# Unread products between the last steps of a four-layer network's kernel, and its final products moved between the steps of a scan

## What is computed

```python
x = L0(x, ctx, mask)        # 16-head attention, feed-forward of 1024
x = L1(ctx, x)              # attention over ctx, a narrow feed-forward of 4, attention on itself
x = L2(x, ctx)              # causal 16-head attention, feed-forward of 1024
# L3: 8-head attention, then a scan over the 128 positions:
x = x + mha(layernorm(x), layernorm(ctx))
u = (layernorm(x) @ W_in.T + b_in) @ Bmat            # 16 x 128 x 64
s_t = silu(s_{t-1} @ A.T) + u_t                      # for t = 0 .. 127, s_{-1} = 0
x = x + s @ Cmat                                     # 64 -> 256
x = x + (programme.mean(axis=1) @ W_prog.T + b_prog)[:, None, :]
```

## Time and profile before

| | |
|---|---|
| median of three runs | 906.49 us |
| the profiled execution's own time | 904.56 us |
| its span, first to last instruction | 902.4 us |
| mean granted clock of TensorE | 0.905 |
| TensorE busy | 762.0 us (84%) |
| VectorE busy | 538.9 us (60%) |
| ScalarE busy | 432.9 us (48%) |
| GpSimd busy | 336.2 us (37%) |
| end of layer C's last drive product to the end | 107 us |

### The profile page before, as it was taken

One profiled execution on the slowest core, in us unless ns is written; L12 is line 12 of the kernel. 1 busy time (PEld: TensorE's weight loads), 2 busy tenths in 40 slices (PEclk: granted clock), 3 DMA queues, 4 the chain that ended last, 5 costly groups with the idle time before them and its releaser, 6 DMA issues.

```text
span 902.4 us, 16307 instructions
## 1 busy us (share of the span) xinstructions
PE 762.0 (84%) x5520; PEld 615.8 (68%) x5520; DVE 538.9 (60%) x2244; ACT 432.9 (48%) x1768; POOL 336.2 (37%) x343
## 2 busy tenths in 40 slices
PE   0699897899799979997999899979899887575556
PEld 0588676688678868886888788857787666344445
DVE  2547678647847884788478947883776473310002
ACT  0635265665553855385538554872465461312221
POOL 3224354434524553454345524652356151100000
PEclk9889998999999999999999999999999889555556
DMA  8400000000000000000000000000000000010002
GB/s 316 179 7 7 24 9 11 4 11 1 19 1 13 1 20 1 13 1 19 1 13 1 14 1 13 1 2 1 1 1 2 0 2 1 0 24 0 1 1 93
DMA packets 14709, 18.73 MB, mean 21 GB/s; under 512 B 3485, under 2 KB 12194, under 8 KB 13986
## 3 DMA queue, kind: packets, MB, share of 16 engines
q1 hardware_dynamic: 14626, 17.69, 6.0%
HBM read 15.59 MB, written 2.10 MB: 20 GB/s over the span
## 4 chain that ended last, share of the span: by engine, by line
PE 68%; DVE 17%; issue 5%; ACT 5%; POOL 3%; DMA 2%; SPq 0%; DVEq 0%; POOLq 0%
PE work_bank L564 21%; PE work_bank L555 20%; PE work_bank L693 6%; PE scores_bank L763 6%; DVE probs L903 4%; DVE probsT L1004 4%; PE work_bank L613 3%; PE work_bank L547 3%; PE scores_bank L591 3%; ACT probs L1145 3%; DVE xn L921 2%; DVE stats L940 1%; DMA bias<-in_mask 1%; ACT probs L1082 1%; POOL probs L786 1%
## 5 line engine op out<-in xcount | busy, mean ns | idle before, releaser
L786 POOL TENSOR_TENSOR probs<-probs,rtotal 128x512 f32<-128x512 f32 x160 | 164.5, 1040 | 219.4 <-DVE rtotal L994 219.1
L1082 ACT ACTIVATE probs<-probs,nmx 128x128 f32<-128x128 f32 x512 | 197.9, 390 | 77.4 <-DVE nmx L903 77.1
L1004 DVE COPY probsT<-work_bank 128x512 f32<-128x512 f32 x160 | 106.4, 679 | 19.2 <-PE work_bank L693 19.0
L693 PE MATMUL work_bank<-ident,probs 128*128 128x128 f32 x640 | 99.2, 296 | 20.9 <-POOL probs L786 14.5
L564 PE MATMUL work_bank<-L_w,hidden 128*128 128x256 f32 x512 | 113.9, 381 | 0.0
L693 PEld LDWEIGHTS work_bank<-ident,probs 128*128 128x128 f32 x640 | 78.2, 151 | 40.5 <-POOL probs L786 21.6
L564 PEld LDWEIGHTS work_bank<-L_w,hidden 128*128 128x128 f32 x512 | 96.0, 190 | 14.1 <-ACT hidden L1137 1.7
L786 POOL TENSOR_TENSOR rstd<-veps,half 128x2 f32<-128x2 f32 x64 | 45.4, 710 | 160.3 <-DVE veps L948 159.9
L1082 ACT ACTIVATION_READ_ACCUMULATOR probs<-probs,nmx 128x1 f32 x512 | 96.7, 189 | 0.0
L763 PE MATMUL scores_bank<-probs,a_t 64*64 64x16 f32 x252 | 49.6, 276 | 33.3 <-ACT probs L1145 33.3
L763 PEld LDWEIGHTS scores_bank<-probs,a_t 64*64 64x64 f32 x252 | 36.0, 203 | 46.8 <-ACT probs L1145 46.8
(11 more groups left out here) (162 smaller groups left out, 1430.7 us busy)
## 6 DMA issues: line engine op xcount, KB each, us to landing
L_w<-in_L_w SPq DMA_DIRECT2D x4, 1024.0 KB, 10.7
x_in<-in_x SPq DMA_DIRECT2D x8, 256.0 KB, 2.8
c_in<-in_ctx SPq DMA_DIRECT2D x8, 256.0 KB, 2.8
out<-x_all SPq DMA_DIRECT2D x8, 256.0 KB, 2.2
rows<-in_rows SPq DMA_DIRECT2D x1, 1280.0 KB, 8.1
bias<-in_mask SPq DMA_DIRECT2D x8, 128.0 KB, 2.2
L_wq<-in_L_wq SPq DMA_DIRECT2D x3, 256.0 KB, 9.6
L_wv<-in_L_wv SPq DMA_DIRECT2D x3, 256.0 KB, 10.1
```

The costliest lines, as they stand in the source:

```text
L693: mm = nc.tensor.transpose(d[:, j * P:j * P + P], src[:, j, :], ident[:])
L786: return nc.gpsimd.tensor_tensor(out, a0, a1, op)
L1004: nc.vector.tensor_copy(turn_slot(s, i, key), d[:].rearrange("p (j k) -> p j k", j=4))\
L1082: ins = nc.scalar.activation(e_at[slot][:, j, :], src, ACT.Exp, bias=nmx[:, slot, j:j + 1], scale=1.0 if s == "C" else -1.0, accum_out=tot ...
```

## The change

1. `occupy` issues products of 128x128 on 128 columns whose results nobody reads. A table `OCCUPIED` puts 8, 2, 8, 8 and 3 of them before C7.flip.x6, C7.q, C7.turn.0, C7.flip.x7 and C7.drive, in the bank which that step then overwrites. In the scan one follows each step before step 99.
2. Of the four L750 products only the first stands before the scan; the others follow steps 8, 40 and 72.
3. The programme is loaded with the weights, last in `REST_LOADS` (into `x7_all`, rows 8 to 11, which are free then). Its means are made with `drive_weight`, and VectorE copies them there.
4. The end's products are split. Positions 0 to 95 ("early") need states up to 95 only: 32 products of 96x128 (`early_part`), one after each step from 99 on, the last three after the scan. For positions 96 to 127 ("late") the batches stand four abreast, 32 partitions each, in a tile `late` (in `probsT`): 32 narrow products (`late_part`) with the inputs and means alone at every fourth step from 13 to 41, and 16 with `w_state` after the last step. SP moves the last 32 rows of `x7_all` into `late` by four transfers.
5. Pairs' stores carry 96 positions and start during the scan; the late ones are four stores, two by SP and two by ScalarE's queue. `w_state` of step 0 is written, and so Silu's table loaded, after C7.out's products.

```diff
@@ pe
+            def occupy(d, n):
+                for _ in range(n):
+                    nc.tensor.matmul(d, wq["L0"][:, 0, 0:P], wk["L0"][:, 0, 0:P], start=True, stop=True,
+                                     skip_group_check=True)
...
+                for b in range(B):
+                    mm = nc.tensor.matmul(d[SS:P, 2 * P + b:2 * P + b + 1], prog[:, b, :], mean_w[:], start=True, stop=True)
                 mm.then_inc(set_up_pe, 1)
...
+                if (s, i, step) in OCCUPIED:
+                    occupy(open_bank(s, i, step)[:, 0:P], OCCUPIED[s, i, step])
...
+            mm = from_u(0)
             for t in range(1, P):
...
                 mm.then_inc(stepped, 1)
+                if t in (8, 40, 72):
+                    from_u(t // 32 + 1)
+                elif t < FROM:
+                    occupy(s_bank[3][:, 3 * P:4 * P] if t < 72 else s_bank[0][:, 0:P], 1)
+                if t == 12:
+                    for w in range(W_BANKS):
+                        pe.wait_ge(drained[w], len(range(w, len(FILLS), W_BANKS)))
+                    pe.wait_ge(late_ready, 1)
+                if 12 <= t < 44 and t % 4 == 1:
+                    late_part((t - 12) // 4)
+                if t >= FROM:
+                    early_part(t - FROM)
+            pe.wait_ge(silued, P - 1)
+            for g in range(4):
+                for j in range(4):
+                    mm = nc.tensor.matmul(s_bank[g // 2][32 * j:32 * j + 32, (g % 2) * D:(g % 2) * D + D],
+                                          w_state[:, EARLY:P, 4 * g + j], w_last[0:SS, :], start=True, stop=True)
+                if g % 2:
+                    mm.then_inc(late_filled, 1)
+            for k in range(P - FROM, 2 * B):
+                early_part(k)
@@ sp
+            sp.wait_ge(*summed_at("C", NT - 1, "x7b"))
+            for j in range(4):
+                sp.dma_start(late[32 * j:32 * j + 32, :, :],
+                             x7_all[EARLY:P, :, :].rearrange("p (g j) d -> p g j d", j=4)[:, :, j, :])\
+                    .then_inc(late_moved, 16)
+            for n in range(NT):
+                sp.wait_ge(last_added, n + 1)
+                sp.dma_start(out[bass.ds(n * PAIR, PAIR), 0:EARLY]..., x7(n)[0:EARLY]).then_inc(out_stored, 16)
+            for j in (0, 1):
+                sp.wait_ge(late_added, 4)
+                sp.dma_start(out[:, EARLY:P]...[j], late[32 * j:32 * j + 32]).then_inc(out_stored, 16)
@@ act
-            act.wait_ge(stepped, 1)
-            nc.scalar.mul(w_state[:, 0, :], u_all[:, 0, :], 0.0)
+            act.wait_ge(*filled_at("C", NT - 1, "out"))
+            nc.scalar.activation(w_state[:, 0, :], zero[:], ACT.Silu)
```

More of the change, by code:

```diff
@@ L245 @@
 W_BANKS, S_BANKS = 4, 4
+EARLY, FROM = 96, 99
+OCCUPIED = {("C", NT - 1, ("flip", "x6")): 8, ("C", NT - 1, ("q",)): 2, ("C", NT - 1, ("turn", 0)): 8,
+            ("C", NT - 1, ("flip", "x7")): 8, ("C", NT - 1, ("drive",)): 3}
 PROBS, TURNED, NORMED, MOMENTS = 6, 6, 3, 4
@@ L500, in _ @@
                     load_x(i)
-            sp.wait_ge(*done("C", NT - 1, "drive"))
-            sp.dma_start(prog, a["prog"].rearrange("b s k -> s b k")).then_inc(prog_loaded, 16)
-            for j in range(NT):
-                sp.wait_ge(last_added, j + 1)
-                sp.dma_start(out[bass.ds(j * PAIR, PAIR)].rearrange("b s d -> s b d"), x7(j)).then_inc(out_stored, 16)
-            sp.wait_ge(out_stored, 16 * NT)
+            sp.wait_ge(*summed_at("C", NT - 1, "x7b"))
[5 more added lines that the diff above has]
+                sp.wait_ge(last_added, n + 1)
+                sp.dma_start(out[bass.ds(n * PAIR, PAIR), 0:EARLY].rearrange("b s d -> s b d"), x7(n)[0:EARLY])\
+                    .then_inc(out_stored, 16)
+            for j in (0, 1):
+                sp.wait_ge(late_added, 4)
+                sp.dma_start(out[:, EARLY:P].rearrange("(g j) s d -> j s g d", j=4)[j], late[32 * j:32 * j + 32])\
+                    .then_inc(out_stored, 16)
+            sp.wait_ge(out_stored, 16 * (NT + 4))
         @block.tensor
@@ new lines, in late_part, with early_part @@
+            def late_part(k):
+                g, lo = k // 2, (k % 2) * P
+                for j in range(4):
+                    mm = nc.tensor.matmul(w_bank[g // 2][32 * j:32 * j + 32, (g % 2) * D + lo:(g % 2) * D + lo + P],
+                                          stT[:, 4 * g + j, EARLY:P], w_last[:, lo:lo + P], start=True, stop=True)
+                if k % 4 == 3:
+                    mm.then_inc(late_filled, 1)
+            def early_part(k):
+                b, lo = k // 2, (k % 2) * P
+                n = b // PAIR
+                if k % 4 == 0:
+                    if n < 2:
+                        pe.wait_ge(states_ready, 3)
+                    elif n < 4:
+                        pe.wait_ge(late_added, n - 1)
+                    else:
+                        pe.wait_ge(last_added, n - 3)
+                at = (b % PAIR) * D + lo
+                mm = nc.tensor.matmul(w_bank[(n + 2) % W_BANKS][0:EARLY, at:at + P], stT[:, b, 0:EARLY],
+                                      w_last[:, lo:lo + P], start=True, stop=True)
+                if k % 4 == 3:
+                    mm.then_inc(last_filled, 1)
@@ L761, in _ @@
+            pe.wait_ge(*done("C", NT - 1, "drive"))
+            mm = from_u(0)
+            for t in range(1, P):
                 if t > 1:
@@ new lines, in _ @@
+            nc.vector.tensor_copy(stT[SS:P, :, :], means[SS:P, :].unsqueeze(2).broadcast_to([SS, B, P]))
+            dve.wait_ge(*done("C", NT - 1, "drive"))
+            nc.vector.tensor_copy(stT[0:SS, :, EARLY:P], u_all[:, EARLY:P, :].rearrange("p t b -> p b t"))\
+                .then_inc(late_ready, 1)
+            for k in range(2):
+                dve.wait_ge(late_filled, k + 1)
+                if k == 0:
+                    dve.wait_ge(late_moved, 16 * 4)
+                nc.vector.tensor_tensor(late[:, 2 * k:2 * k + 2, :], by_batch(w_bank[k]), late[:, 2 * k:2 * k + 2, :],
+                                        ALU.add).then_inc(late_added, 1)
@@ new lines, in add_late @@
+            def add_late(k):
+                dve.wait_ge(late_filled, k + 3)
+                if k == 0:
+                    dve.wait_ge(late_added, 2)
+                nc.vector.tensor_tensor(late[:, 2 * k:2 * k + 2, :], by_batch(s_bank[k]), late[:, 2 * k:2 * k + 2, :],
+                                        ALU.add).then_inc(late_added, 1)
+            whole = (P - FROM) // 4
+            for n in range(whole):
+                add_early(n)
+            for k in range(2):
+                add_late(k)
@@ L1059, in _ @@
+            for n in range(whole, NT):
+                add_early(n)
         @block.scalar
@@ L1146, in _ @@
                     .then_inc(silued, 1)
+            for j in (2, 3):
+                act.wait_ge(late_added, 4)
+                nc.scalar.dma_start(out[:, EARLY:P].rearrange("(g j) s d -> j s g d", j=4)[j],
+                                    late[32 * j:32 * j + 32]).then_inc(out_stored, 16)
 def _columns(inputs):
```

65 lines of the change are left out of this document (23 added, 42 removed).

## The result

The changed kernel takes 942.97 us (median of 5 runs, 937.11 to 943.88) against 904.61 of the kernel before in the same comparison (903.1 to 906.86): **1.0406 times as long, interval 1.0377 to 1.0435**. The profiled execution took 937.11, its span is 935.2 (902.4 before, +32.8). The forecast was 877.4, with a range of 870 to 893. In all ratios of this document a run more than 1.5% above the fastest of its kernel is left out as slow; that is one run, of the fifth experiment.

What follows compares the result with a forecast made beforehand. TensorE was taken to be busy near full clock for most of the span, then some 120 us set by one chain of waits at 1.2 GHz. Six terms summed to -28.1 us, giving 877.4 us, range 870 to 893.

Steps and rivals of the forecast that it cites:

- term 3: Scan steps: each takes 0.56 us instead of 0.66 at 2.4 GHz, its unread product costing nothing; -12.6 us.
- rival E: Scan steps: each weight load waits behind the unread product, 0.23 us longer 124 times at 1.2 GHz; 928 us; chance 0.06.
- clock up from the last flip to the end: Last pair's flip through scan to end: TensorE stays at 2.4 GHz, the likeliest case; 870 to 882 us; chance 0.57.
- B: Last flip through scan: clock lost in part, half of the steps at 0.66 us; about 887 us; chance 0.14.
- Term 1: Last pair: unread products keep 2.4 GHz for query product (-1.7 us) and for flip and drive product (-1.3).
- Term 2: Start of the scan: only the first L750 group stays in front, 1.35 us instead of 10.5; -9.15 us.
- Rival D: Scan steps: clock up, but a lone pass hardly shortens, gaining 0.03 us a step instead of 0.10; 886 us; chance 0.08.
- Term 4: Work inserted in scan steps: three L750 groups at 0.4 us each, eight narrow groups at 0.1 each; +2.0 us.
- Term 5: End after the last Silu: split products and early stores make it 7.1 us instead of 13.2; -6.1 us.
- Term 6: Mid-run, programme means made with `drive_weight`: 32 more passes partly covered and one small copy; +0.7 us.

Runs made afterwards that it cites:

- run 5: The fifth experiment: whole change with scan stationary zero-padded to 128x128, early parts 128x128, step product 128 columns; 920.47 us, 1.0152 of the kernel before.
- run 6: Changed kernel with end behind the scan again, scan stationary padded to 128x128, 128x128 product of 128 columns in nearly every step; 923.07 us, 1.02 of before.
- run 12: run 4 with scan stationary still 64x64, plus a step product of 128x64 on 128 columns; 885.49 us, 0.9764 of the kernel before.
- run 1: Changed kernel without the unread product in the scan steps; 907.79 us, 1.0019 of the kernel before.
- run 2: Changed kernel with the step's unread product in the scan's shape, 64x64, still 128 columns; 910.27 us, 1.0042 of the kernel before.
- run 4: Changed kernel without step products and with the end behind the scan as in the kernel before; 898.02 us, 0.9934 of before.
- run 10: Changed kernel with end behind the scan, scan stationary row-padded to 128x64, step product 128x64 on 128 columns; 880.1 us, 0.971 of the kernel before.
- run 8: run 4 also without the unread products of the last pair (`OCCUPIED` empty); 902.81 us, 0.998 of the kernel before.
- run 13: Whole change, scan and step product 128x64, 128 columns, each early part as two 128x64 products; 881.34 us, 0.9707 of the kernel before.
- run 11: Whole change, scan and step product 128x64, 192 columns, early parts still 128x96; 890.49 us, 0.9795 of the kernel before.
- run 7: run 6 with 192 instead of 128 columns in each step's product; 895.24 us, 0.989 of the kernel before.
- run 3: Changed kernel with the step's unread product still 128x128 but 16 columns instead of 128; 928.27 us, 1.0242 of the kernel before.

## Why the prediction was wrong

**The step that failed** is the sentence in term 3 on the product in each step: "at 2.4 GHz its two passes are through 0.36 us after the step's start, 0.2 before the next begins: no cost". The second pass is out of the array 0.71 us after it (797.98 to 798.69), and the next load waits for that, to 0.63; I had counted streaming alone, and one load behind another. I took the distance of passes from places where one shape follows itself, and rival E was dismissed for the same reason ("back-to-back passes with different stationaries now follow at streaming pace"): the words hold for different stationaries of one shape. For two shapes my own said otherwise, and I did not read them so: L763's first pass (64x64) comes 0.17 behind L758's last (128x64), which follow each other every 0.107, and 0.07 before that one's end. E had the right place and the right kind of wait, but only one wait of 0.22 where there are two, and a share of 0.06; it gave 928 (its sum of the four pieces is 0.69, not the 0.67 written there, which would be 0.25 a step and 931).

At 2.4 GHz that alone would have been small: 0.63 is below the 0.66 of before, and 95 steps of 0.63 instead of 0.56 are 7 us (an estimate from these steps), which leaves the forecast inside its range. The loss needed the second failure, the forecast's condition itself, "clock up from the last flip to the end". TensorE counted as busy all through, yet the clock fell 13 us into the scan, and at 1.2 GHz the same product costs 0.39 a step. So B, with nearly all of the scan at the lower clock, came together with E. Why the clock fell stays open: it also fell in runs 5 and 6, where no shape changes, and it stayed in run 12, where the shape does.

*Term 1*, last pair -3.0: right in some executions. Flip and drive fell by 1.2 (forecast 1.3); the query product did not (3.79, forecast 1.73), and the score products behind it took 2.12 instead of 1.21 in this execution. In the traces of runs 1, 2, 4 and 10, with the same code up to the scan or nearly so, the query product took 2.0 and the whole pair 33.0 us, -2.7; in the others with these products it took 3.6 to 3.8 and the pair 34.3 to 34.8, and without them (run 8) 3.8 and 36.9. So the eight products in front of the flip hold the clock through the query product at times, not each time.

*Term 2*, scan's start -9.15: right, -9.1; without a product in the first step (run 1) it is 1.36, the 1.35 of the sum.

*Term 3*, the step itself: right in size. ScalarE starts 0.11 earlier at 2.4 GHz, 0.10 was forecast; the first seven steps of runs 1 and 4 have it without any product (0.55), and run 10's 71.1 us are 126 steps of 0.555 and 1.3 for the three groups. Rival D does not hold here: 0.11 was gained, not 0.03. The rule of the Trainium skill behind it (TensorE: Matmul & The Clock Gate, "Single matmul latency") that a lone product's fixed part hardly moves is given there for one bf16 product; for these fp32 products of two passes the traces say otherwise. Run 5 shows a load with twice the columns to be 0.05 us longer each at 2.4 GHz, run 6 0.10 at 1.2. By the same page ("LDWEIGHTS") 64 more columns are 0.053 us, with no other figure for the lower clock (an estimate from it): the traces agree at 2.4 GHz and not at 1.2.

*Term 4*, +2.0, of which 1.2 for the three groups and 0.8 for the narrow ones. The three groups cost 1.26 each at 1.2 GHz (steps of 1.92 instead of 0.66 in run 4) and 0.43 each at 2.4 (0.98 instead of 0.555 in run 10), 1.3 in all: right. The narrow groups cost 0.29 each beside steps of 128x64 (run 13 against run 10, 2.3 in all), and 0.36 at 2.4 and 0.58 at 1.2 GHz in the changed kernel: the 0.1 was too small, for their stationary of 128x32 changes the shape as well. Not forecast at all: an early part beside a scan step at 1.2 GHz costs 0.33, the same wait and length as the product.

*Term 5*, -6.1: -3.3, at 1.2 GHz. Run 13, with the clock held, has 7.8 us against the forecast 7.1, so -5.5.

*Term 6*, +0.7: from the end of the products in front of `drive_weight` to layer B's first score it is 3.74 us instead of 3.29, +0.45, and +0.4 to +0.9 in the other runs' traces: right. That the end of ffn2 comes 0.7 later says less, since it moves by 3 us between traces of the same code.

So the sum was within 4 us of what the whole idea gives in one shape and with the clock held (run 13, 881.3), in part by luck: the narrow groups cost 1.5 more than forecast and the end 0.7 more, the steps 0.6 less. What was wrong was to take the product's shape as free and the clock as kept.

## What to carry to other kernels

Before putting filler products, or real ones, between the steps of a serial chain on TensorE, give them the shape (rows and columns) of the chain's own stationary, padding the chain's rows with zeros if the filler is to have 128 rows (0.555 us a step with 128x64, as fast as the 0.55 of 64x64 alone); a padding in columns has to be loaded each time (0.66 with 128x128). Look in the trace for the distance between the last pass of one shape and the next load of another: it is not the distance of equal ones. And cost a filler at both clocks, since the clock it is to hold is the one that makes it fit.

## What the runs showed of the hardware

- A load with a new shape started 0.07 to 0.08 us before the earlier pass was out, at both clocks and in all three kinds of change: rows and columns (changed kernel), rows (run 12), columns (run 11 at 854.64: the early part's load 0.22 behind the step's start). With equal shapes it started 0.22 before in L633 of the kernel before, and 0.24 in run 2, where it waited for ScalarE. That the array has to be empty for it is my reading; the ends are modelled, and the delays between starts (0.21 instead of 0.11, run 12 against run 10) are what was measured.
- What TensorE did while the clock held or fell, in the profiled executions: products of 128 rows and 128 columns, clock at 2.4 GHz all through in steps of 0.555 and 0.58 us (runs 10, 12), fallen after 9 to 33 us in steps of 0.63 and 0.66 (changed kernel, runs 5, 6); with 192 columns in steps of 0.66 it stayed (run 7); with 64 rows and 128 columns it fell after 4 us (run 2), as it did without products (runs 1, 4). TensorE counted as busy all through in every one of these with products. These are single places, and no rule that tells them apart is shown here.
- A filler's cost is not its columns: at 1.2 GHz 16 columns with the wrong shape cost 0.20 us a step (run 3), 128 with the right one nothing (run 2). At 2.4 GHz the 16 columns cost nothing either (0.55 in run 3's first steps), and 128 with the wrong shape 0.08 (0.63).
